# A Haar-wavelet attention block on one core: channel maxima moved from TensorE to VectorE, and half of the residual adds moved from accumulating DMAs to the engines

## What is computed

```
ll, lh, hl, hh = haar_dwt(x)                     # 80x80 each
fused = relu(bn1(conv1x1(concat(ll, lh, hl, hh), fusion_w, fusion_b)))   # 1024 -> 256
avg_sp = mean(fused, axis=channels);  max_sp = max(fused, axis=channels)
spatial_out = sigmoid(conv7x7(concat(avg_sp, max_sp), sa_w)) * fused
avg_ch = mean(spatial_out, axis=pixels);  max_ch = max(spatial_out, axis=pixels)
ch_map = sigmoid(mlp(avg_ch) + mlp(max_ch))
projected = relu(bn2(conv1x1(ch_map * spatial_out, proj_w, proj_b)))     # 256 -> 1024
out = haar_idwt(split4(projected)) + x
```

## Time and profile before

| | |
|---|---|
| median of 3 runs | 2600.19 us (2592.7 to 2600.36) |
| the profiled execution | 2597.0 us, of which 2595.1 us are its span from the first to the last instruction |
| PE busy | 2469.7 us, 95% of the span |
| DVE busy | 1994.8 us, 77% |
| ACT busy | 1077.9 us, 42% |
| POOL busy | 355.2 us, 14% |
| mean granted TensorE clock | 0.984 |

### The profile page before, as it was taken

One profiled execution on the slowest core, in us unless ns is written; L12 is line 12 of the kernel. 1 busy time (PEld: TensorE's weight loads), 2 busy tenths in 40 slices (PEclk: granted clock), 3 DMA queues, 4 the chain that ended last, 5 costly groups with the idle time before them and its releaser, 6 DMA issues. The chain is left out here.

```text
span 2595.1 us, 32968 instructions
## 1 busy us (share of the span) xinstructions
PE 2469.7 (95%) x12996; PEld 2200.7 (85%) x12996; DVE 1994.8 (77%) x2560; ACT 1077.9 (42%) x1413; POOL 355.2 (14%) x346
## 2 busy tenths in 40 slices
PE   4999999999999999999999999999999999987874
PEld 3888889898898989989898988989899898976764
DVE  4656777798778887798777987788877987787875
ACT  2445534354344533354434543345333453334221
POOL 0100111111111111111111111111111111111110
PEclk9999999999999999999999999999999999998897
DMA  3445699999999999999999999999999999898999
GB/s 125 157 147 195 185 267 262 257 297 270 256 270 273 287 261 260 250 304 271 265 266 256 303 263 261 262 280 286 260 259 263 295 268 267 242 248 237 277 272 245
DMA packets 115178, 659.91 MB, mean 254 GB/s; under 512 B 19520, under 2 KB 20560, under 8 KB 115024
## 3 DMA queue, kind: packets, MB, share of 16 engines
q1 hardware_dynamic: 82768, 448.07, 48.8%
q0 software_dynamic: 32256, 209.73, 41.6%
HBM read 447.83 MB, written 209.92 MB: 253 GB/s over the span
## 5 line engine op out<-in xcount | busy, mean ns | idle before, releaser
L375 PE MATMUL pp<-y_hi,wp_hi 128*128 128x480 f32 (+1 forms) x1792 | 674.5, 376 | 59.1 <-DVE y_lo L676 35.8
L615 DVE TENSOR_TENSOR x_lo<-xin,x_hi 128x1920 fp32r<-128x1920 f32 (+1 forms) x224 | 474.0, 2116 | 302.3 <-ACT x_hi L463 302.2
L389 PE MATMUL pf<-x_hi,wf_hi 128*128 128x480 f32 (+1 forms) x1792 | 676.4, 377 | 6.5 <-ACT fused L536 3.5
L375 PE MATMUL pp<-y_lo,wp_hi 128*128 128x480 f32 (+1 forms) x1792 | 670.6, 374 | 0.0
L375 PE MATMUL pp<-y_hi,wp_lo 128*128 128x480 f32 (+1 forms) x1792 | 669.0, 373 | 0.0
L389 PE MATMUL pf<-x_lo,wf_hi 128*128 128x480 f32 (+1 forms) x1792 | 664.5, 371 | 0.0
L389 PE MATMUL pf<-x_hi,wf_lo 128*128 128x480 f32 (+1 forms) x1792 | 664.3, 371 | 0.0
L463 ACT ACTIVATE x_hi<-xin 128x1920 fp32r<-128x1920 f32 (+1 forms) x224 | 418.5, 1869 | 572.1 <-PE pf L389 572.1
L659 DVE SCALAR_TENSOR_TENSOR xout<-sd,both 128x960 f32<-128x960 f32 (+1 forms) x448 | 504.8, 1169 | 49.2 <-DMA out_dram<-xout 41.9
L492 ACT ACTIVATE relu<-pp,t 128x480 f32<-128x480 f32 (+1 forms) x448 | 286.3, 642 | 390.4 <-PE pp L375 349.0
L375 PEld LDWEIGHTS pp<-y_hi,wp_hi 128*128 128x128 f32 x1792 | 341.9, 191 | 110.0 <-DVE y_lo L676 40.6
(11 more groups left out here) (82 smaller groups left out, 1117.2 us busy)
## 6 DMA issues: line engine op xcount, KB each, us to landing
xin<-in_x_dram SPq DMA_DIRECT2D x160, 960.0 KB, 8.3
xout<-in_x_dram POOLq DMA_DIRECT2D x160, 960.0 KB, 10.9
out_dram<-xout SPq DMA_DIRECT2D x160, 960.0 KB, 11.8
xin<-in_x_dram SPq DMA_DIRECT2D x64, 800.0 KB, 7.5
xout<-in_x_dram POOLq DMA_DIRECT2D x64, 800.0 KB, 10.7
out_dram<-xout SPq DMA_DIRECT2D x64, 800.0 KB, 11.0
sigb<-sig_scratch SPq DMA_DIRECT2D x64, 400.0 KB, 8.1
fused<-in_L_conv_fusion_w_dram SPq DMA_DIRECT2D x1, 1024.0 KB, 4.9
```

The lines of the kernel that those rows point to most:

```text
L375: mm = pe.matmul(pp[j][:, 0:n_px], w[:, kt, cols], y[:, s.pc, kt, 0:n_px], start=(kt == 0 and m == 0), stop=(kt == CT - 1 and m == 2))
L389: mm = pe.matmul(pf[o][:, 0:n_px].rearrange("p (y w) -> p y w", w=W2), w[:, i, q, o * P:(o + 1) * P], v[:, q % 2, :, q // 2, :], start=(i ...
L615: nc.vector.tensor_tensor(halves(x_lo, i, k), pairs(i, k), halves(x_hi, i, k).bitcast(F32), ALU.subtract).then_inc(xlo_ready[i], 1)
```

## The change

- **Channel maxima.** PE's transposes of `mx` go. DVE transposes `mx` in blocks of 32x32 (`turn`) and reduces each block to 32 maxima (`blockmax`); once per image PE turns `blockmax` with two transposes, DVE reduces it (`spatial_max`), and the map goes through DRAM into `maps` (two small DMAs).
- **Channel sums.** They stay on PE as one fp32 matmul per row, but with operands exchanged: `pick` (32 columns) is the stationary operand and the row of `sm` (80 columns) is streamed. They move from the middle of a slot to its end (`add_channels`). POOL makes `sm` one slot later, and only after `x_lower(k+1, 0)`. The convolution moves from the end of phase 0 to phase 1.
- **EXTRA is 7.** The gating slots are phases 2 to 5, `LAST` is 7; slots 0 to 20 hold a fusion alone, slots 112 to 132 a projection alone.
- **Adding x.** `adding(kc, i)` says which output halves still get x by an accumulating DMA: the half i = 1 outside the tail, and both halves in gating slots. The others get x by a plain load into `xre` (three buffers), and DVE and POOL each add one half of the pixels from `cell` (`residual`). In the tail all halves go this way.
- **Start.** The vectors are loaded as rows of 128 values and turned by one PE transpose. The projection's weights and the MLP's are prepared after slot 0 (`prepare_late`).
- **Last image.** Its map is loaded by two DMAs into the free `xin` and `x_hi` (`last_gate`).

The core of the diff:

```diff
-EXTRA = 6
+EXTRA = 7
...
-        xout = sb("xout", [P, 4, XPM])
+        xre = sb("xre", [P, 3, XPM])
...
-        GATED = {1: (0, 1), 2: (2, 3), 3: (4, 5), 4: (6, 7)}
+        GATED = {2: (0, 1), 3: (2, 3), 4: (4, 5), 5: (6, 7)}
...
+        def adding(kc, i):
+
+            return kc + LAG < NT and (i == 1 or (kc + LAG) % TILES in GATED)
...
+        def residual(eng, ops, kc, i, hand, added):
+
+            g = 2 * kc + i
+            n = 2 * px_of(kc)
+            part_of = slice(hand * n, (hand + 1) * n)
+            eng.wait_ge(xre_landed[g % 3], 16 * uses(g, False))
+            eng.wait_ge(cell_ready, 2 * (g + 1))
+            x_part = xre[:, g % 3, part_of]
+            ops.tensor_tensor(x_part, x_part, cell[:, part_of], ALU.add).then_inc(added, 1)
...
             def channel_sum(s):
...
+                k = s.k - 1
+                n = px_of(k)
+                gp.wait_ge(f_ready, CT * (k + 1))
+                if s.load_next:
+                    gp.wait_ge(xlo_ready[0], s.k + 2)
+                need(gp, sum_psum, k)
...
-                for r in range(rows):
-                    pe.transpose(pm[0:W2, r * P:(r + 1) * P], mx[:, r * W2:(r + 1) * W2], ident[:, :])
-                for r in range(rows):
-                    mm = pe.matmul(pm[0:W2, MEANS + r:MEANS + r + 1], sm[:, r * W2:(r + 1) * W2],
-                                   ones[:, 0:1], start=True, stop=True)
-                mm.then_inc(t_psum, 1)
+                for r in range(ROWS[k % TILES]):
+                    row = FIRST[k % TILES] + r
+                    at, base = row % GROUP, row - row % GROUP
+                    m = min(GROUP, H2 - base)
+                    mm = pe.matmul(sums[base:base + m, :], pick[:, GROUP - 1 - at:GROUP - 1 - at + m],
+                                   sm[:, r * W2:(r + 1) * W2], start=(at == 0), stop=(at == m - 1))
+                mm.then_inc(sum_psum, 1)
...
+            def turn(s):
+
+                block, px, n = span_of(s.k)
+                blocks = -(-n // GROUP)
+                dve.wait_ge(mx_ready, s.k + 1)
+                need(dve, blockmax_ready, s.k)
+                nc.vector.transpose(turned[:, 0:blocks * GROUP], mx[:, 0:blocks * GROUP]).then_inc(turned_ready, 1)
+                dve.wait_ge(turned_ready, s.k + 1)
+                need(dve, across_psum, s.b)
+                nc.vector.tensor_reduce(blockmax[:, block:block + blocks],
+                                        turned[:, 0:blocks * GROUP].rearrange("p (n c) -> p n c", c=GROUP),
+                                        AX.X, ALU.max).then_inc(blockmax_ready, 1)
```

More of the change, by code:

```diff
@@ L63, in haar_block @@
     PAD = KS // 2
[L64 removed]
     NK = 2 * KS
+    GROUP = 32
     FIRST = [sum(ROWS[:t]) for t in range(TILES)]
@@ L429, in body @@
-                if s.c:
+                elif s.c:
                     pe.wait_ge(lo_ready, CT * (s.kc + 1))
                     project(s, 0)
-                if s.phase != LAST:
-                    if s.turn:
-                        turn(s)
-                    if s.a:
-                        fusion(s, 1)
+                if s.a:
+                    fusion(s, 1)
+                if s.phase == 0:
+                    pe.wait_ge(blockmax_ready, s.k)
+                    for h in range(2):
+                        n = NPX // GROUP // 2
+                        mm = pe.transpose(across[:, h * P:(h + 1) * P], blockmax[:, h * n:(h + 1) * n], ident[:, :])
+                    mm.then_inc(across_psum, 1)
@@ L437, in body @@
+                if s.phase == 1 and s.a:
+                    convolve(s)
+                if s.phase == LAST:
+                    pe.wait_ge(lo_ready, CT * (s.kc + 1))
+                    project(s, 0)
                 if s.c:
                     project(s, 1)
-                if s.phase == 0:
-                    pe.wait_ge(map_ready, 2 * s.k)
-                    pe.wait_ge(band_pass, KS * NK)
-                    for j in range(NK):
-                        mm = pe.matmul(pm[0:H2, 0:W2], maps[:, j // KS, j % KS:j % KS + H2], band[:, j, :],
-                                       start=(j == 0), stop=(j == NK - 1))
-                    mm.then_inc(conv_psum, 1)
+                if s.turn:
+                    add_channels(s)
@@ L453, in body @@
                     mm.then_inc(hid_psum, 1)
-            for s in slots:
+            body(slots[0])
+            prepare_late()
+            for s in slots[1:]:
                 body(s)
@@ L544, in body @@
                     relus(s, 1)
-            for s in slots:
+                if s.phase == 1 and not s.a:
+                    spatial_gate(s)
+            body(slots[0])
+            prepare_late()
+            for s in slots[1:]:
                 body(s)
@@ L719, in body @@
                     nc.vector.tensor_reduce(pool[:, :, 1], part[:, 1, :, :], AX.X, ALU.max).then_inc(pool_ready, 1)
-                if ahead and s.turn:
-                    spatial(s)
                 if s.phase in GATED:
```

388 lines of the change are left out of this document (251 added, 137 removed).

## The result

The changed kernel takes 2576.8 us (median of 4 runs, 2576.41 to 2577.79), the one before 2599.02 us (4 runs beside it): a ratio of 0.9924, 95% interval 0.99 to 0.9949. That is 0.8% faster. The forecast was 2527 us, its range 2506 to 2566: **too optimistic by 50 us, outside the range**. The profiled execution has a span of 2574.7 us.

A forecast was written before the change was run, and what follows sets the result against it. PE bounds the middle stretch, DVE and DMAs lie close in the tail. Tail start 2279.4 - 56 + 2 + 3 - 10.5 - 8 + 3.5 - 4 = 2209, plus 316 of tail, plus 1.9: 2527 us, range 2506 to 2566.

The forecast's parts named there:

- Who could be late now?: Middle stretch: DVE at 21.15 us stays just under PE's 21.9 us gating slot; 3 us lost in the whole stretch.
- I take 0: Channel sums on PE: the exchanged operands cost no extra time, 0.07 us apart as before.
- The transposes' 0.65 us, -56 us: Middle stretch: dropping PE's transposes, 5 or 6 per slot at 0.108 us, saves 56 us over 91 slots.
- EXTRA, -10.5 us: Slot 20 loses its projection, 48 matmuls, so the tail begins 10.5 us earlier; they are paid again in the tail.
- The first stretch: Fusion-alone slots go from 12.47 to 12.05 us, -8 us over 20 slots, with +2 and +1.5 us against it.
- The start, -4 us: Start: short vector loads and later weight preparation save a net 4 us, bounds -9 and +2.
- DVE's transpose and reduction: DVE's new block transpose and reduction of 480 elements in a slot: 0.65 us each.
- The tail: Projection-alone slots at the end: DVE is the limit, 13.65 us per slot of 6 rows, 316 us in all.
- Gating slots bound by DVE: Rival: DVE sets gating slots at 23 us, +25 to +45 us, 2550 to 2572 us; chance 0.15.
- Tail hand-overs: Rival: buffer hand-overs or POOL's slipped halves, not DVE's sum, bind the tail: 2545 to 2580 us; chance 0.20.
- Slow sums: Rival: weights and stream do not overlap in the new sums, 0.165 us more each, +211 us, 2738; chance 0.03.
- The tail begins later than 2225 us: Sign that the prediction is wrong; it had the tail begin at 2209 us.

The follow-up runs named there:

- Experiments 4: Changed kernel with the discarded output of ACT's chunk means in its own buffer instead of on `relu`, two waits removed: 2552.18 us.
- experiment 5: Changed kernel with the chunk means' output in its own buffer and, in phase 7, DVE's `turn` ahead of the second `x_lo`: 2544.33 us.
- experiment 6: Changed kernel with x added by accumulating DMA in both halves in phases 6 and 7 too: 2570.85 us.
- experiment 3: Changed kernel with DVE computing `y_lo` ahead of the next `x_lo` in phase 7: 2567.56 us.
- experiment 2: Changed kernel with the sums' stationary side 80 columns wide instead of 32, one group over the whole image instead of three: 2556.57 us.
- experiment 7: Changed kernel with the tail's x added by accumulating DMAs in both halves, as before the change: 2600.52 us.
- experiment 10: Kernel of experiment 8 with every fourth half tile of the tail getting x by accumulating DMA: 2562.31 us.
- experiment 8: Changed kernel with 80-column sums, own output for the means, and in phase 7 `y_lo` and channel gate ahead of `x_hi`/`x_lo`, `turn` ahead of second `x_lo`: 2522.22 us.
- experiment 11: The changed kernel itself, unaltered, measured once more: 2576.96 us.
- experiment 9: Kernel of experiment 8 with the tail's plain adds split 3/8 to DVE and 5/8 to POOL instead of half and half: 2523.47 us.

## Why the prediction was wrong, point by point

- **"Who could be late now?" (the step that failed).** It asked whether DVE's work fits into a slot, took one gating slot and one without gating, both with 6 rows, and said of the second "DVE has 16.89 us of work and gets the added half as well, about 1.1 us: no danger". For slots of 6 rows that held: gating slots have DVE busy for 20.21 us of 22.14 and PE never waits. It failed in two ways. First, the last gating slot was not summed. EXTRA moved it to 5 and 5 rows: 18.65 us of PE against a round of DVE of 21.0 us, and DVE enters phase 6 late by 1.9 to 3.5 us more than it entered phase 5. Second, in phases 6 and 7 the work is a chain through all engines (means, `pool`, squeeze, excite, logit, `ch`, `y_hi`, `y_lo`), in which DVE idles 4.1 us for ACT. There a load sum does not tell; the distance does between the time at which a result is there and the time at which PE wants it. It was 0.64 us before. Against it came the late start, 2.2 us of new work ahead of the logit (`turn` and the add), 0.77 us of POOL's sum in `y_lo`, and a slot of phase 6 that PE leaves 1.1 us earlier where it does not stop. In place of no wait, PE stopped for 3.0 to 3.5 us in each of six images. Experiments 4 and 5 give the price of the whole: the tail began at 2227.8 us in place of 2260.8, 33 us. About 24 of these are PE's waits (1975.13 - 1948.88 = 26.3 us, less the 2.6 that stay in experiment 5), the other 9 us are busy time that went with the low clock. The shares are not shown one by one: the add alone was worth 6 us (experiment 6), `y_lo` ahead of `x_lo` 9 (experiment 3), and no run moved POOL's sum alone or gave the last gating slot its old length.
- **"I take 0" for the new form of the sums (a term of the wrong size).** The spacing of 0.07 us, read off the convolution, was right. The edges were not priced: 0.23 to 0.25 us per slot, 20 us over the stretch by experiment 2. The convolution's row could not have shown it: its stationary side is 80 columns, wide like the old sums.
- **The transposes' 0.65 us, -56 us**: right. With the edges mended a slot is 21.89 to 21.91 us (21.9 was forecast), and the stretch 1921.6 (1922.2).
- **"92 slots"** in the middle stretch are 91: its window begins with slot 21. The -56 us were worked out for 91, so no term moves.
- **EXTRA, -10.5 us**: slot 20 went from 21.36 to 11.26 us, -10.1.
- **The first stretch**: slots 2 to 19 lost 4.8 us, 4.5 were forecast for 0 to 19. Fusion-alone slots are 12.1 us (12.05).
- **The start, -4 us**: slot 2 begins at 62.25 in place of 67.89 us, -5.6. The first DVE work is at 7.75 us (about 9 was forecast), the first fusion matmul at 27.30 instead of 42.94; of these 15.6 us 10 are given back in slots 0 and 1, as the work behind slot 0 stands in the open.
- **DVE's transpose and reduction**: 0.67 and 0.65 us, 0.65 forecast for each.

```profile
L849 DVE STREAM_TRANSPOSE sd<-sd 128x480 f32<-128x480 f32 x80 | 53.7, 672 | 0.0
L852 DVE TENSOR_REDUCE blockmax<-sd 128x15 f32<-128x480 f32 x80 | 52.2, 653 | 2.7
```

- **The tail**: slots of 13.49 us (13.65), DVE busy for 13.19 of 13.50, a DMA share of 0.82 (0.8), 313.9 us in all (316). Image 7's chain keeps PE for 7.8 us (7). Experiment 7 shows the gain against the old way, 23.7 us by the medians.
- **The rivals.** Gating slots bound by DVE: false where it was priced, for slots of 6 rows; the last gating slot, with 5, does put DVE behind, and PE pays two slots later. Tail hand-overs: not in the changed kernel, but real in experiment 10. Slow sums: a small part of it, 0.24 us per slot and not 0.165 per sum. "The tail begins later than 2225 us" was named as what would make the prediction wrong, and it did. So did "PE waits for `y_lo` behind gating slots", two slots behind.

The order by which `y_lo` and `ch` could come sooner still (experiment 8 against 2 and 5 together) is worth 1 to 2 us at most, within the error. What decides whether a stop is followed by the low clock stays open.

## What to carry to other kernels

Sum the work for every kind of slot, the shortest above all, and do it anew when an offset like EXTRA pairs other tiles. After that, look for the one or two stages in which the bounding engine needs a result of the same stage, and measure there how long the result has been there before it is wanted: that slack (0.64 us here), not the engine's idle time, is what new work and a faster bound use up. A scratch output that nobody reads can be the link that makes such a chain wait. When work is moved on one engine, look at what it now lies beside on the others: moved behind `x_lo`, POOL's sum met `y_lo`. When a matmul's form is changed, price its edges to the neighbours beside its own spacing, and where a wait is removed, look for the next one before promising its length.

## What the runs showed of the hardware

- Between matmuls with 128 stationary columns, a group with 32 costs PE 0.23 to 0.25 us per round trip at its edges; one with 80 costs nothing measurable, with plain fp32 among fp32r matmuls and 80 or 1 streamed columns.
- The granted clock after a stop is not settled by the stop's length: in experiment 11 stops of 3.45 to 3.46 us were followed by 6.8 us at half clock in two slots, and by none in two others of the same execution; in experiment 6 stops of 2.57 to 2.69 us by 3.4 us in five slots and by nothing in one; in experiment 3 those of 1.0 to 1.7 us were followed by none, one of 1.8 us by 3.4 us. Beside a stop of the same length without it, a slot with the low clock took 1.1 us more, since a wait behind it was covered.
- In the changed kernel a `y_lo` pass of 480 elements took 0.71 us in all 131 cases without arithmetic of POOL beside it (the longest 0.716), and up to 2.70 us with it; `mx` of 416 elements, 0.59 us alone, took up to 1.92. The `sd` passes, which read PSUM, never changed (0.70 to 0.72 us). The `x_lo` passes never lay beside POOL's arithmetic there, but in the kernel before they did, and the rows show both ways: begun behind POOL's sum, an `x_lo` of 2.15 us took up to 3.14; begun 0.2 us ahead of it, it kept 2.15 and POOL's sum of 1.22 us took 3.0. A row of each (kernel before):

```profile
523.90 3.13 DVE L615 TENSOR_TENSOR x_lo<-xin,x_hi 128x1920 fp32r<-128x1920 f32 x1 [0.24 <-ACT x_hi L463]
501.87 3.01 POOL L314 TENSOR_TENSOR sm<-fused 128x480 f32<-128x480 f32 x1 [5.28 <-issue]
```

The Trainium skill (SBUF — State Buffer, SBUF: two separate sides) has an exclusive lock between DVE operations with two SBUF inputs and GpSimd's that read SBUF, held by the one that starts first. These rows of `x_lo`, `y_lo` and `mx` agree, and in experiment 9 the add grew by 0.13 and 0.33 us where it shared 0.26 and 0.47 us with POOL's. Seven `y_lo` passes of the kernel before do not fit: they took 2.28 to 2.41 us, though their rows begin 0.4 us ahead of POOL's sum.
